# Layer 0 attention of a four-layer conditioned transformer: value and output weights folded, inputs double-buffered, blocks written out

## What is computed

```
h = film(rmsnorm(x, norm1_w), cond, film1_w, film1_b)     # x*(1+scale)+shift, per sequence
Q, K, V = h @ q_w + q_b, h @ k_w + k_b, h @ v_w + v_b
attn = softmax(Q K^T * 256**-0.5)                         # 64x64 for each sequence
x = x_in + (attn @ V) @ proj_w + proj_b
```

## Time and profile before

| what | us |
| --- | --- |
| median of 3 runs | 2225.43 |
| lowest run | 2223.94 |
| the profiled execution | 2222.83 |
| its span | 2221.0 |
| first projection of layer 0's attention starts | 28.38 |
| first `down` matmul of layer 0's MLP starts | 218.62 |

### The profile page before, as it was taken

How to read it: one execution, slowest core, us unless ns; L and a number is a source line. 1 busy time by engine, 2 the same in 40 slices (tenths; PEclk the granted TensorE clock), 3 DMA queues, 4 the chain that set the end, 5 groups by cost and what they waited for, 6 DMA issues and landing times.

```text
span 2221.0 us, 45198 instructions
## 1 busy us (share of the span) xinstructions
PE 2087.0 (94%) x15856; PEld 1692.9 (76%) x15856; DVE 1344.9 (61%) x2570; ACT 997.9 (45%) x1608; POOL 407.9 (18%) x425
## 2 busy tenths in 40 slices
PE   5889999999999999999999999998899999999998
PEld 4777788777777778787777777776688787787887
DVE  4564665667767565654555544546766677775664
ACT  2443455545444333334444444444344555554443
POOL 1121211223222010110112111112511222220000
PEclk9999999999999999999999999999999999999999
DMA  5000000000000000000000000000000000000000
GB/s 213 10 14 9 8 11 7 15 8 14 7 14 10 10 19 9 19 10 11 7 6 5 0 5 5 5 1 13 5 7 5 10 10 10 5 5 1 28 19 29
DMA packets 17855, 33.30 MB, mean 15 GB/s; under 512 B 1266, under 2 KB 11762, under 8 KB 17138
## 3 DMA queue, kind: packets, MB, share of 16 engines
q1 hardware_dynamic: 17778, 32.25, 4.5%
HBM read 28.06 MB, written 4.19 MB: 15 GB/s over the span
## 4 chain that ended last, share of the span: by engine, by line
PE 76%; DVE 10%; issue 8%; ACT 3%; POOL 2%; DVEq 0%; DMA 0%; ACTq 0%; SPq 0%; POOLq 0%
PE psum L541 20%; PE psum L543 19%; PE psum L542 19%; PE psum L632 4%; PE psum L645 3%; PE psum L578 2%; PE psum L665 2%; PE psum L731 2%; PE psum L679 1%; PE psum L621 1%; DVE xn L1010 1%; DVE h_lo L1030 1%; PE psum L498 1%; DVE hm L1020 1%; DVE hm L1025 1%
## 5 line engine op out<-in xcount | busy, mean ns | idle before, releaser
L541 PE MATMUL psum<-h_hi,w_lo 128*128 128x512 f32 x1152 | 479.7, 416 | 28.2 <-DVE h_lo L1030 21.6
L543 PE MATMUL psum<-h_hi,w_hi 128*128 128x512 f32 x1152 | 457.9, 398 | 0.0
L542 PE MATMUL psum<-h_lo,w_hi 128*128 128x512 f32 x1152 | 457.7, 397 | 0.0
L1141 DVE TENSOR_TENSOR hid_lo<-hid,hid_hi 128x512 fp32r<-128x512 f32 x256 | 201.7, 788 | 263.2 <-ACT hid_hi L896 262.9
L541 PEld LDWEIGHTS psum<-h_hi,w_lo 128*128 128x128 f32 x1152 | 218.8, 190 | 85.4 <-issue 25.8
L896 ACT ACTIVATE hid_hi<-hid 128x512 fp32r<-128x512 f32 x256 | 161.9, 632 | 225.7 <-PE psum L543 134.7
L543 PEld LDWEIGHTS psum<-h_hi,w_hi 128*128 128x128 f32 x1152 | 218.1, 189 | 53.8
L542 PEld LDWEIGHTS psum<-h_lo,w_hi 128*128 128x128 f32 x1152 | 218.7, 190 | 42.1
L1082 DVE TENSOR_REDUCE mx<-psum 128x8 f32<-128x512 f32 x192 | 132.4, 690 | 160.6 <-PE psum L621 107.3
L891 ACT ACTIVATE hid<-psum,vec 128x512 f32<-128x512 f32 x192 | 131.9, 687 | 199.9 <-PE psum L543 197.9
L541 PE MATMUL psum<-hid_hi,w_lo 128*128 128x512 f32 x512 | 202.8, 396 | 5.8 <-DVE hid_lo L1141 3.9
(11 more groups left out here) (118 smaller groups left out, 3717.3 us busy)
## 6 DMA issues: line engine op xcount, KB each, us to landing
stage<-in_w_dram SPq DMA_DIRECT2D x24, 256.0 KB, 2.7
stage<-in_w_dram SPq DMA_DIRECT2D x8, 512.0 KB, 3.5
out_dram<-xres SPq DMA_DIRECT2D x8, 512.0 KB, 2.9
xres<-in_x_dram SPq DMA_DIRECT2D x1, 3584.0 KB, 18.9
modw_mod<-in_modw_dram SPq DMA_DIRECT2D x2, 1536.0 KB, 13.8
stage<-in_w_dram SPq DMA_DIRECT2D x8, 384.0 KB, 3.3
stage<-in_w_dram SPq DMA_DIRECT2D x8, 192.0 KB, 2.4
modw_film<-in_modw_dram SPq DMA_DIRECT2D x1, 1024.0 KB, 6.9
```

The lines of the kernel that those rows point to most:

```text
L541: nc.tensor.matmul(dst, s_lo, m_hi, start=start and j == 0, stop=False)
L542: nc.tensor.matmul(dst, s_hi, m_lo, start=False, stop=False)
L543: ins = nc.tensor.matmul(dst, s_hi, m_hi, start=False, stop=stop and j == len(pairs) - 1)
L1141: nc.vector.tensor_tensor(hid_lo[:, slot, :], hid32[:, slot, :], hid_hi[:, slot, :].bitcast(F32), ALU.subtract).then_inc(sem["hid"], 1)
```

## The change

- The host-laid value and output weights are multiplied on the chip at the start: PE transposes `wv` and forms wv @ wo, and a bias row v_b @ wo + o_b (`fold_vo`, eight fp32 matmuls, six of 256 and two of 128 columns); ACT and DVE split the product into the place of the value weights (`folded`). `v` now yields V @ proj_w, `pv` yields attn @ V @ proj_w with tokens on the partitions, in four matmuls of 256 columns. `proj`, the eight transposes of `back`, their ACT evacuations and the split of the attention output are gone.
- The bias row is added to `xres` by POOL in a new stage `bias` (128x1024, in place), and DVE's `back` adds PSUM into `xres` behind it.
- h has two buffers (`h_of`: even blocks h_hi/h_lo, odd blocks at_hi/at_lo), the values too (`v0_sb[b % 2]`).
- All eight blocks of this phase are written out, with no loop.
- The stages stand in a new order, `stats` first; `exp` is a stage of its own late in the block; `divide`, `probs_t`, `pv` and `back` belong to the block before.
- POOL adds the shift in layer 0's attention too.
- In all phases eps is added by DVE inside an instruction that was there already, and POOL's L1228 is gone, 64 times in all.
- The table parts and the first `up` stages of the MLP stand at other places. Two small loads and their waits are new at the start.

The diff, cut to its core:

```diff
-DOWN = {(kind, layer): (8 if kind == "mlp" or layer == 2 else 2) * D for kind, layer in PHASES}
+DOWN = {(kind, layer): (8 if kind == "mlp" or layer == 2 else 2 if layer else 0) * D for kind, layer in PHASES}
...
-        return [prev("probs_t"), nxt("stats"), own("scores"), prev("pv"), nxt("norm"), own("v", 0), own("v", 1),
-                nxt("turn"), nxt("split"), prev("proj"), nxt("q", 0), nxt("q", 1), prev("back"), nxt("k", 0),
-                nxt("k", 1), own("divide"), own("share")]
+        return [nxt("stats"), prev("divide"), own("q", 0), own("q", 1), own("k", 0), nxt("norm"), own("k", 1), prev("probs_t"),
+                own("bias"), nxt("turn"), prev("pv"), prev("back"), nxt("split"), own("scores"), own("v", 0), own("v", 1),
+                own("exp"), own("share")]
...
-TABLE_AFTER = [("pv", 0), ("v", 0), ("v", 1), ("proj", 0), ("back", 0), ("share", 0)]
+TABLE_AFTER = [("q", 0), ("k", 0), ("pv", 0), ("scores", 0), ("v", 0), ("v", 1)]
...
-UP_AFTER = {0: [("pv", 0), ("proj", 0)], 1: [("merge", 0), ("proj", 0)],
+UP_AFTER = {0: [("probs_t", 0), ("pv", 0)], 1: [("merge", 0), ("proj", 0)],
...
-        c.update(q=2, k=2, v=2, w_full=3, w_free=1, att_hi=2, att=2)
+        c.update(q=2, k=2, v=2, w_full=1, out_rows=0, biased=1)
...
-        v0_sb = place("v0_sb", [P, TILES, D], F32, free + 12288)
+        v0_sb = [place(f"v0_sb{n}", [P, TILES, D], F32, where) for n, where in enumerate((free + 12288, wb + 45056))]
...
+        def h_of(ph, b):
+
+            return (at_hi, at_lo) if ph == 0 and b % 2 else (h_hi, h_lo)
...
-                if engine is None:
+                if engine is None or ph == 0:
...
-            return PHASES[ph] in (("attn", 1), ("attn", 3))
+            return PHASES[ph] in (("attn", 0), ("attn", 1), ("attn", 3))
...
+            if of == 0:
+                last -= 1
...
-            sp.dma_start(w0_staged_sb[:, :], weights_in[0]).then_inc(w0_staged, 16)
+            w0_up = weights_in[0][:, 0:UP["attn", 0]].rearrange("p (c n) -> p c n", c=DC)
+            w0_down = weights_in[0][:, UP["attn", 0]:UP["attn", 0] + DC * D].rearrange("p (c n) -> p c n", c=DC)
+            sp.dma_start(w0_staged_sb[:, :, :], w0_up[:, :, 0:QK0]).then_inc(w0_staged, 16)
+            sp.dma_start(wv[:, :, :], w0_up[:, :, QK0:QK0 + D]).then_inc(vo_loaded, 16)
+            sp.dma_start(wo[:, :, :], w0_down).then_inc(vo_loaded, 16)
...
+            pe.wait_ge(vo_loaded, 32)
+            for kc in range(DC):
+                for m in range(DC):
+                    ins = nc.tensor.transpose(psum[:, W_BANK, kc * D + m * P:kc * D + (m + 1) * P], wv[:, m, kc * P:(kc + 1) * P],
+                                              ident)
+            ins.then_inc(vo_turned, 1)
...
+            def fold_vo():
+
+                pe.wait_ge(wv_t_done, 1)
+                pe.wait_ge(vo_cols, 2)
+                for m in range(DC):
+                    for kc in range(DC):
+                        nc.tensor.matmul(psum[:, W_BANK, m * D:(m + 1) * D], wv_t[:, kc, m * P:(m + 1) * P], wo[:, kc, :],
+                                         start=kc == 0, stop=kc == DC - 1)
+                for kc in range(DC):
+                    nc.tensor.matmul(psum[:, W_BANK + 1, 0:D], vo_col[:, kc, :], wo[:, kc, :], start=kc == 0, stop=False)
+                for m in range(DC):
+                    ins = nc.tensor.matmul(psum[:, W_BANK + 1, m * P:(m + 1) * P], vo_col[:, DC + m, :], ident,
+                                           start=False, stop=m == DC - 1)
+                ins.then_inc(vo_product, 1)
+
...
+                if s == "split" and ph == 0 and is_first(b):
+                    fold_vo()
+                if s == "v" and ph == 0 and k == 0 and is_first(b):
+                    pe.wait_ge(vo_ready, 1)
...
-                    for m in range(DC):
-                        for t in range(TILES):
-                            ins = nc.tensor.matmul(wide[:, m, t * P:(t + 1) * P], v0_sb[:, t, m * P:(m + 1) * P],
-                                                   pt[:, 0, t * P:(t + 1) * P], start=True, stop=True)
+                    for t in range(TILES):
+                        ins = nc.tensor.matmul(wide[:, t // 2, (t % 2) * D:(t % 2 + 1) * D], pt[:, 0, t * P:(t + 1) * P],
+                                               v0_sb[b % 2][:, t, :], start=True, stop=True)
...
-                elif s == "back":
+                elif s == "back" and ph:
...
+            for kc in range(DC):
+                where = slice(kc * 3 * D, kc * 3 * D + QK0)
+                nc.scalar.activation(w_hi[0][:, where], w0_staged_sb[:, kc, :], ACT.Copy).then_inc(w0_hi_done, 1)
+            act.wait_ge(vo_turned, 1)
+            nc.scalar.activation(wv_t[:, :, :], psum[:, W_BANK, :].rearrange("p (c n) -> p c n", c=DC),
+                                 ACT.Copy).then_inc(wv_t_done, 1)
...
+                if s == "q" and ph == 0 and k == 0 and is_first(b):
+                    act.wait_ge(vo_product, 1)
+                    nc.scalar.activation(folded(w_hi[0]), psum[:, W_BANK, :].rearrange("p (c n) -> p c n", c=DC),
+                                         ACT.Copy).then_inc(vo_hi_done, 1)
...
-                elif s == ("exp" if layer == 2 else "scores"):
+                elif s == "exp":
...
-                elif s in ("pv", "merge") and (layer == 0 or s == "merge"):
+                elif s == "merge":
                     act.wait_ge(sem["w_full"], n_at("w_full", ph, b, 1))
                     for m in range(DC):
-                        if layer == 0:
-                            src = wide[:, m, :]
-                            dst = at_hi[:, m, :]
-                        else:
-                            src = wide.rearrange("p w (g h q) -> p (w g) h q", h=2, q=S)[:, :, m, :]
-                            dst = by_seq(at_hi[:, m, :])
-                        nc.scalar.activation(dst, src, ACT.Identity, bias=col(f"v{layer}", m)).then_inc(sem["att_hi"], 1)
+                        src = wide.rearrange("p w (g h q) -> p (w g) h q", h=2, q=S)[:, :, m, :]
+                        nc.scalar.activation(by_seq(at_hi[:, m, :]), src, ACT.Identity,
+                                             bias=col(f"v{layer}", m)).then_inc(sem["att_hi"], 1)
                 elif s == "pv" and layer == 2:
...
-                elif s == "proj" and layer in (0, 1):
+                elif s == "proj" and layer == 1:
...
+            def folded_lo():
+
+                dve.wait_ge(vo_product, 1)
+                nc.vector.tensor_copy(vo_bias[:, :], psum[:, W_BANK + 1, 0:D]).then_inc(vo_cols, 1)
+                dve.wait_ge(vo_hi_done, 1)
+                nc.vector.tensor_tensor(folded(w_lo[0]), psum[:, W_BANK, :].rearrange("p (c n) -> p c n", c=DC),
+                                        folded(w_hi[0]).bitcast(F32), ALU.subtract).then_inc(vo_ready, 1)
...
-                        nc.vector.tensor_tensor(ms[:, :], ms[:, :], mv[:, :, 1], ALU.add).then_inc(sem["rstd_in"], 1)
-                    else:
-                        nc.vector.tensor_copy(ms[:, :], mv[:, :, 1]).then_inc(sem["rstd_in"], 1)
+                        nc.vector.scalar_tensor_tensor(ms[:, :], ms[:, :], EPS[layer], mv[:, :, 1], ALU.add,
+                                                       ALU.add).then_inc(sem["rstd_in"], 1)
+                    else:
+                        nc.vector.tensor_scalar(ms[:, :], mv[:, :, 1], EPS[layer], None, ALU.add).then_inc(sem["rstd_in"], 1)
...
-                elif (s == "pv" and layer == 0) or s == "merge":
+                elif s == "merge":
...
-                        last = 3 if layer != 2 else 1
+                        last = 3 if layer in (1, 3) else 1
+                        if layer == 0:
+                            dve.wait_ge(sem["biased"], n_at("biased", ph, b, 1))
...
-                    nc.gpsimd.tensor_tensor(ms[:, :], ms[:, :], eps_t[:, layer, :], ALU.add).then_inc(sem["eps_added"], 1)
-                    pool.wait_ge(sem["eps_added"], n_at("eps_added", ph, b, 1))
                     nc.gpsimd.tensor_tensor(rstd[:, :], ms[:, :], half_t[:, :], ALU.pow).then_inc(sem["rstd"], 1)
...
+                elif s == "bias":
+                    if is_first(b):
+                        pool.wait_ge(vo_cols, 3)
+                    pool.wait_ge(sem["normed"], n_at("normed", ph, b, 1))
+                    xs = xres[:, bass.ds(b * TILES, TILES), :]
+                    nc.gpsimd.tensor_tensor(xs, xs, vo_bias[:, :].unsqueeze(1).to_broadcast([P, TILES, D]),
+                                            ALU.add).then_inc(sem["biased"], 1)
```

More of the change, by code:

```diff
@@ L151, in counts_of @@
 def counts_of(kind, layer):
-    c = dict(stats_raw=1, stats=1, mean_sq=1 if layer < 2 else 0, rstd_in=1, rstd=1, normed=1, eps_added=1, modded=2,
+    c = dict(stats_raw=1, stats=1, mean_sq=1 if layer < 2 else 0, rstd_in=1, rstd=1, normed=1, modded=2,
              h_hi=2, h=2, out_rows=2, x_done=1)
@@ L435, in last_h_reader @@
                 return sem[name], n_at(name, ph, b, 0)
```

(27 more changed lines are left out.)

52 lines of the change are left out of this document (31 added, 21 removed).

## The result

The changed kernel takes 2185.93 us, the median of four runs from 2181.89 to 2190.35, against 2223.94 us for the kernel before, the median of its three runs without the one of 4509.24 us: a ratio of 0.9829, with a 95% interval of 0.9811 to 0.9846. That is 38 us less, 1.7%. The profiled execution took 2190.35 us (span 2188.6), where 2189.1 had been forecast for it. It is the slowest of the four.

A forecast was written before the change was run, and what follows sets the result against it. A DVE chain that PE waits on bounds the block: 28.4 + 15.2 + 6 x 16.6 + 42.7 = 185.9 against 218.62, plus 1 us for eps, gives 2189.1 profiled, 2191 median; range 2171 to 2206.

The forecast's parts named there:

- norm held by divide and bias: Layer 0's attention blocks: VectorE's xn scalings wait behind POOL's two instructions, ending at 5.6 us after stats.
- The block, busy time: One layer 0 attention block: PE 13.2 us, DVE 9.8, POOL about 8.4, with 2.4 for the bias addition.
- The port: DVE and POOL's shared port: locked for a whole instruction, free between two; norm ends at 5.5 or, without gaps, 5.8.
- One xn between: Between POOL's divide and bias: one xn scaling of 0.3 us perhaps gets the port.
- The loop: Middle blocks of layer 0's attention, timed from stats' end to the next: 16.3 us, 16.6 with half at 1.2 GHz.
- PE's wait ahead of the turn: Middle blocks: PE idles about 3 us before each turn, waiting for xn; 2 to 4 us was the sign.
- w_lo fell between the lo halves: POOL's w_lo (1.27 us) falls between DVE's lo halves, ending at 12.4 instead of 11.3; less overlap at 1.2 GHz.
- The clock: Middle blocks: PE's pauses lower its clock, so pv runs at 1.2 GHz in half the blocks, 1.8 us longer.
- The first block: Start of layer 0's attention: q and k 8 us, partly at 1.2 GHz; next q 15.2 us after the first.
- The last block: End of layer 0's attention: first `down` 42.7 us after q, with PE idle 4.6 waiting for divide.
- The PE-bound case: Rival: the port costs nothing, loop 13.2 to 13.5 us, time 2172 us; chance 0.18.
- The slower loop: Rival: norm waits for both POOL instructions, every pv at 1.2 GHz; 18.5 us a block, 2202 us; chance 0.17.

The follow-up runs named there:

- the first two experiments: Changed kernel with GpSimd's bias addition left out, 2170.11 us; changed kernel with the bias stage moved to the head of the order, 2173.84 us.
- the kernel with the added wait: Changed kernel with bias at the head, softmax division moved to VectorE's back, and bias waiting for the block's two lo halves: 2169.55 us, ratio 0.9753.
- the four kernels that reach it: Changed kernel without bias, 2170.11; bias first, 2173.84; bias first, division on VectorE and bias waiting for lo halves, 2169.55; that with earlier table parts, 2170.66 us.
- one-buffer: Changed kernel with a single buffer for the input h instead of two: 2215.10 us, ratio 0.9953.
- shift-on-DVE: Changed kernel with layer 0's shift addition back on VectorE: 2192.47 us, ratio 0.9864.

## Why the prediction was right, step by step

The time came out 5 us under the 2191 that was forecast, and the profiled execution within 1.3 us of 2189.1. That agreement is in part luck: 6.7 us that the rebuilt stretch gained beyond the forecast stand against about 7 us lost later that nothing had foreseen, in a trace that is the slowest of four runs. The mechanism, norm held by divide and bias, came as forecast, and the first two experiments show it.

- **The block, busy time.** PE 13.2 forecast, 13.1 measured at full clock; POOL 8.4 against 8.3 to 8.7; bias 2.4 against 2.42. DVE's 9.8 can't be compared with the 12 to 13 measured, since a held instruction is counted as busy.
- **The port.** "One xn between" divide and bias is just what the durations 1.13, 2.46, 0.34, 0.34 show. The Trainium skill (SBUF — State Buffer, "SBUF: two separate sides") has the lock held for a whole instruction, so that it is free between two; here the trace agrees, other than at the two memsets of the earlier trace rows, which let nobody in. The scaling in between delayed the bias by next to nothing (2.42, against 2.40 in the kernel with the added wait, where nothing held it).
- **The loop.** With zero at DVE's end of stats (90.98): divide ends at 2.1 (2.1 forecast), bias at 4.5 (4.7), the turn starts at 5.2 (5.7), pv at 6.2 (6.55), back ends at 9.4 (10.0), the next stats at 15.7 (16.3). Almost all of the 0.6 comes from the bias and from norm's remainder. PE's wait ahead of the turn had been put at about 3 us, with 2 to 4 as the sign; it was 1.3 to 2.4, and two of the six lie below 2. w_lo fell between the lo halves in the three blocks whose pv ran at full clock (the pair takes 2.38) and not in the three at 1.2 GHz (1.29 to 1.42), as forecast.
- **The clock.** Half of the pv at 1.2 GHz: three of six, after pauses of 2.36, 2.37 and 2.34, none after the 1.27 and the 1.39, and none after one more pause of 2.37. From q to q the six blocks took 96.3 us, 16.05 each, against 16.6.
- **The first block** was mis-sized: 11.8 us from q to q in place of 15.2. q and k ran at full clock (5.8, not 8), and the next q followed v directly at 39.42, since the lo halves were done 0.05 before. Some of it came back at once: the block behind it took 17.9 from q to q, with a pause of 2.36 and a piece at 1.2 GHz, the five after that 15.7 each.
- **The last block** took 43.5 us from q to first down, against 42.7, with the pause of 4.17 us before the last probs_t where 4.6 was forecast.
- **In sum**: 0.8 (first q at 27.6), 3.4, 3.3 and -0.8 make the 6.7.
- **Moved work at no cost.** Unrolling was in the sum at nothing. In the changed kernel that held: layer 2's loop has the 15 instruction packets that it had before. But the risk wasn't named, and in the kernel before the same edit alone cost 27 us. What lengthens layer 2's attention by 2.1 us after is neither eps (491.9) nor a reload of instructions.
- **The rivals.** The PE-bound case was priced right: 2172 forecast, 2169.6 to 2173.8 for the four kernels that reach it. It simply wasn't this kernel. The slower loop is the neighbourhood of the one-buffer and the shift-on-DVE kernels.

## What to carry over

Before an elementwise operation is moved to GpSimd, look at what VectorE does in those microseconds: beside VectorE's PSUM reads it held nothing up in these runs, beside operations on SBUF alone it stopped them, and one entry further along the queue or one added wait was worth 12 or 13 us here. After each such move find where the GpSimd instruction lands now, because it takes its collision with it. And when code is written out, compare the later phases too, since a long loop elsewhere can start to reload its instructions.

## What the runs showed of the hardware

- A loop on PE that nobody touched took 492.0, 508.8 or 521.8 us, with 15, 33 or 51 packets on the instruction queue. Putting 128 instructions ahead of it took one kernel from 521.8 to 492.0 us and another from 494.3 to 508.8. Each nine packets more came with two pauses of PE at the top of the loop's body (1.8 to 2.6 us each), in four blocks or in two, and the mean granted clock of the phase was 0.97 at 51 packets, against 0.99 with the 128 instructions ahead. The Trainium skill (Runtime: NRT & Kernel Launch, "Instruction fetch mechanics") says that a taken branch out of the loaded window makes the engine wait for a fetch, and prefers unrolling. The place of the pauses agrees with the first, though not every return to the top pauses; the second failed here, where unrolling another phase brought them on.
- 128 semaphore increments on PE put its first matmul off by 14.4 us (26.37 in place of 12.00). They could start when `vec` had landed, at 6.88, so by an estimate from these times one took 0.11 to 0.15 us, and a part lay under the wait for the tables.
- Between two VectorE instructions that come right behind one another a waiting GpSimd instruction gets the port: the lo pair, 1.3 us of work, took 3.89 with the bias in it.
- In layer 1's attention, identical code got one, two, three or five pieces of 3.4 us at 1.2 GHz in the traces of different kernels, at about 1.25 us each. What sets the number is open.
